# A seven-product linear layer with low-rank adapters: weight differences moved to GpSimd, loads of the first phase spread, and four smaller edits

## The reference

```python
result = jnp.einsum('bsd,od->bso', x, base_weight) + base_bias
A = lora_A_w[adapter_ids]
Bw = lora_B_w[adapter_ids]
h = jnp.einsum('bsd,brd->bsr', x, A)
lora_out = jnp.einsum('bsr,bor->bso', h, Bw)
result = result + lora_out
...
x = x + _L0_cond_ref(x, itok_B_6_15, L0_cond_base_weight, ...)
```

## Time and profile before

| | before |
|---|---|
| median of three runs | 1349.38 us |
| the profiled execution, its own time | 1349.27 us |
| its span, first to last instruction | 1347.5 us |
| mean granted TensorE clock | 0.994 of full |
| TensorE (matmul) busy | 1317.5 us, 98%, 7136 matmuls |
| VectorE busy | 594.5 us, 44% |
| ScalarE busy | 223.4 us, 17% |
| GpSimd busy | 191.9 us, 14% |
| DMA, mean over the span | 229 GB/s |

### The profile page before, as it was taken

One profiled execution on the slowest core, in us unless ns is written; L12 is line 12 of the kernel. 1 busy time (PEld: TensorE's weight loads), 2 busy tenths in 40 slices (PEclk: granted clock), 3 DMA queues, 4 the chain that ended last, 5 costly groups with the idle time before them and its releaser, 6 DMA issues.

```text
span 1347.5 us, 18275 instructions
## 1 busy us (share of the span) xinstructions
PE 1317.5 (98%) x7136; PEld 1208.9 (90%) x7136; DVE 594.5 (44%) x831; ACT 223.4 (17%) x408; POOL 191.9 (14%) x98
## 2 busy tenths in 40 slices
PE   7999979999999999999999999999999999999998
PEld 7999879999998888899999999999988888888886
DVE  4244345444545444564343645434644345533321
ACT  4111122111122000121111212111311111201110
POOL 0000012222220000022444522122100000000000
PEclk9999989999999999999999999999999999999999
DMA  5347767777688777746668755675566778855552
GB/s 199 130 151 264 235 240 283 265 257 255 237 274 287 249 253 266 295 161 239 240 240 301 268 202 151 196 217 194 177 231 237 252 257 299 291 188 196 197 193 102
DMA packets 93513, 308.78 MB, mean 229 GB/s; under 512 B 10482, under 2 KB 19746, under 8 KB 93474
## 3 DMA queue, kind: packets, MB, share of 16 engines
q1 hardware_dynamic: 93474, 308.35, 66.8%
HBM read 211.82 MB, written 97.01 MB: 229 GB/s over the span
## 4 chain that ended last, share of the span: by engine, by line
PE 87%; DMA 5%; DVE 4%; SPq 2%; ACT 1%; issue 1%; POOL 0%; DVEq 0%; ACTq 0%
PE acc L915 31%; PE acc L928 28%; PE acc L921 26%; PE acc L962 2%; DMA pool<-xT 2%; SPq L395 1%; DMA pool<-wT 1%; DVE h_keep L745 1%; DVE h_cols L751 1%; DMA w_sums<-pool 1%; DMA w_raw<-w_sums 1%; SPq L457 1%; POOL pool L854 0%; PE turned L951 0%; ACT x_hi L580 0%
## 5 line engine op out<-in xcount | busy, mean ns | idle before, releaser
L928 PE MATMUL acc<-w_lo,x_hi 128*128 128x352 f32 (+2 forms) x2304 | 566.0, 344 | 0.0
L928 PEld LDWEIGHTS acc<-w_lo,x_hi 128*128 128x128 f32 x2304 | 404.2, 189 | 33.2
L915 PE MATMUL acc<-w_hi,x_hi 128*128 128x352 f32 x1536 | 336.3, 327 | 19.9 <-DVE keep L780 11.7
L915 PE MATMUL acc<-w_hi,x_lo 128*128 128x352 f32 x1536 | 332.2, 324 | 0.0
L915 PEld LDWEIGHTS acc<-w_hi,x_hi 128*128 128x128 f32 x1536 | 258.9, 190 | 20.7 <-issue 12.4
L915 PEld LDWEIGHTS acc<-w_hi,x_lo 128*128 128x128 f32 x1536 | 264.6, 189 | 0.0
L921 PE MATMUL acc<-w_hi,x_hi 128*128 128x512 f32 x768 | 242.0, 396 | 0.1
L686 DVE TENSOR_TENSOR x_lo<-pool,x_hi 128x1024 fp32r<-128x1024 f32 x110 | 142.2, 1293 | 220.9 <-ACT x_hi L580 220.7
L921 PE MATMUL acc<-w_hi,x_lo 128*128 128x512 f32 x768 | 239.6, 392 | 0.0
L580 ACT ACTIVATE x_hi<-pool 128x1024 fp32r<-128x1024 f32 x110 | 116.2, 1056 | 706.8 <-PE acc L928 398.6
L786 DVE TENSOR_TENSOR pool<-acc,pool 128x352 f32<-128x352 f32 (+2 forms) x176 | 102.5, 635 | 184.6 <-PE acc L962 182.0
(11 more groups left out here) (35 smaller groups left out, 413.4 us busy)
## 6 DMA issues: line engine op xcount, KB each, us to landing
pool<-xT SPq DMA_DIRECT2D x142, 512.0 KB, 6.0
pool<-x SPq DMA_DIRECT2D x64, 512.0 KB, 5.7
out<-pool SPq DMA_DIRECT2D x48, 512.0 KB, 2.8
pool<-wT SPq DMA_DIRECT2D x32, 512.0 KB, 7.0
w_sums<-pool SPq DMA_DIRECT2D x32, 512.0 KB, 3.6
w_raw<-w_sums SPq DMA_DIRECT2D x32, 512.0 KB, 5.6
s_sums<-pool SPq DMA_DIRECT2D x32, 512.0 KB, 8.2
pool<-s_sums SPq DMA_DIRECT2D x32, 512.0 KB, 5.6
```

Of the source, the lines that this page charges most:

```text
L915: mm = nc.tensor.matmul(acc[j][:, o, 0:COLS_A], xs, w_hi[:, s, base + o * COLS_A:base + (o + 1) * COLS_A], start=(k == 0 and part == 0), s ...
L928: mm = nc.tensor.matmul(acc[j][:, o, low:low + n], x_hi[:, j, k], w_lo[:, slot(ph, k), first:first + n], start=False, stop=end and (ph not ...
```

## The change

Six edits:

1. The sets start at tile 2 + 3n instead of 4 + 3n, and all four differences are taken on GpSimd, the three behind `add_out` of their tile.
2. The pieces have a table of their own for when they are loaded and stored (`PIECE_LOAD`); each store follows the load by one tile.
3. The first four W chunks of the next phase are loaded one a tile, in tiles 11 to 14 of a phase, ahead of the set's loads.
4. In P1, P6 and P5 VectorE's `step` begins with the read-out of the tile before; it stood behind the splits of x and A.
5. The high and low columns of A change places (`HI_AT`, `LO_AT`), so that x_lo's product with the bank of the A columns can leave out the 16 low ones (336 columns instead of 352).
6. TensorE starts with 24 products of the unit matrix by itself. The last tile is written out: its `turn` and `low_rank` come after its chunks 5 and 6, its last chunk goes bank by bank, and each bank is read out and stored by itself.

```diff
+HI_AT = (RANK, AC + HALF)
+LO_AT = (0, AC + HALF + RANK)
-PREP_FROM = 4
+PREP_FROM = 2
+WARM = 24
+PIECE_LOAD = {(P1, 1): 0, (P1, 3): 1, (P1, 6): 2, (P1, 9): 3, (P1, 12): 4,
+              (P4, 2): 5, (P4, 4): 6, (P4, 6): 7, (P4, 8): 8}
+PIECE_SPLIT = {(ph, t + 1): n for (ph, t), n in PIECE_LOAD.items()}
+LAST_TURN, LAST_LORA = 5, 6
...
@@ SP, step(tile)
                 load_out(tile)
+                early = row(tile) - (2 * PEELED - 1)
+                if ph + 1 < len(PHASES) and 0 <= early < AHEAD:
+                    load_w_first(ph + 1, early)
                 chunk, part = prep_at(tile)
...
-                if j == 0 and piece_at(tile) is not None:
-                    load_piece(piece_at(tile))
+                if (ph, row(tile)) in PIECE_LOAD:
+                    load_piece(PIECE_LOAD[ph, row(tile)])
...
-                if ph + 1 < len(PHASES):
-                    load_w_first(ph + 1)
...
+            def store_last():
+                b = OUT_AT[P3][1][0]
+                for o in range(2):
+                    at = slice(o * BANK, (o + 1) * BANK)
+                    sp.wait_ge(acc_read, place(LAST) + o + 1)
+                    sp.dma_start(out[row(LAST):row(LAST) + 1, :, HALF + o * BANK:HALF + (o + 1) * BANK],
+                                 pool[:, b, at]).then_inc(pool_out[b], DMA)
@@ VectorE, step(tile)
+                if place(tile) and back.ph not in LORA_PHASES:
+                    read_out(back)
...
-                if place(tile):
+                if place(tile) and back.ph in LORA_PHASES:
                     read_out(back)
...
-                if prep_at(tile)[1] == 1:
-                    prep(prep_at(tile)[0])
@@ GpSimd (prep itself as on VectorE, with gp. and nc.gpsimd.)
                 if ph in ADD_PHASES:
                     add_out(tile)
+                if prep_at(tile)[1] == 1:
+                    prep(prep_at(tile)[0])
                 if prep_at(tile)[1] == 2:
                     prep_last(prep_at(tile)[0])
@@ TensorE
+                        ends = part == 1 and o == H_BANK[j]
+                        low, high = (0, COLS_A)
+                        if ends:
+                            low, high = (RANK, COLS_A) if j == 0 else (0, COLS_A - RANK)
+                        mm = nc.tensor.matmul(acc[j][:, o, low:high], xs,
+                                              w_hi[:, s, base + o * COLS_A + low:base + o * COLS_A + high],
...
+            def last():
+                back = after(LAST, -1)
+                begin(LAST)
+                for k in range(KC - 1):
+                    chunk(LAST, k)
+                    if k == TURN_AFTER:
+                        turn(back)
+                    if k == LORA_AFTER:
+                        low_rank(back)
+                    if k == LAST_TURN:
+                        turn(LAST)
+                    if k == LAST_LORA:
+                        low_rank(LAST)
...
+            pe.wait_ge(eye_filled, 3)
+            for _ in range(WARM):
+                nc.tensor.matmul(turned[:, 0:P], eye[:], eye[:], start=True, stop=True)
```

More of the change, by code:

```diff
@@ L525, in step @@
                     prep_store_last(chunk)
-                if j == 1 and piece_at(tile) is not None:
-                    store_piece(piece_at(tile))
+                if (ph, row(tile)) in PIECE_SPLIT:
+                    store_piece(PIECE_SPLIT[ph, row(tile)])
                 if tile == Tile(P1, 3, 0):
@@ L648, in step @@
                     h_high(tile)
-                if j == 1 and piece_at(tile) is not None:
-                    piece_high(piece_at(tile))
+                if (ph, row(tile)) in PIECE_SPLIT:
+                    piece_high(PIECE_SPLIT[ph, row(tile)])
                 if i >= PEELED and ph + 1 < len(PHASES):
@@ L809, in step @@
                     x_low(one)
-                if prep_at(tile)[1] == 1:
-                    prep(prep_at(tile)[0])
                 if ph in (P7, P3):
                     h_low(tile)
-                if j == 1 and piece_at(tile) is not None:
-                    piece_low(piece_at(tile))
+                if (ph, row(tile)) in PIECE_SPLIT:
+                    piece_low(PIECE_SPLIT[ph, row(tile)])
                 if i >= PEELED and ph + 1 < len(PHASES):
@@ L843, in _, with prep @@
                             step(Tile(ph, i, j))
[L844 removed]
+            b = OUT_AT[P3][1][0]
+            dve.wait_ge(pool_in[b], DMA * (LOADS[P3][b] + PAIRS))
+            for o in range(2):
+                rows = pool[:, b, o * BANK:(o + 1) * BANK]
+                dve.wait_ge(last_done, o + 1)
+                nc.vector.tensor_tensor(rows, acc[1][:, o], rows, ALU.add).then_inc(acc_read, 1)
         @block.gpsimd
         def _(gp):
+            def prep(n):
+                a, b, c = PREP_AT
+                gp.wait_ge(pool_in[a], DMA * (2 * n + 1))
+                gp.wait_ge(pool_in[b], DMA * (n + 1))
+                nc.gpsimd.tensor_tensor(pool[:, a], pool[:, b], pool[:, a], ALU.subtract).then_inc(w_summed, 1)
+                gp.wait_ge(pool_in[c], DMA * (n + 1))
+                gp.wait_ge(w_summed, 4 * n + 1)
+                nc.gpsimd.tensor_tensor(pool[:, b], pool[:, c], pool[:, b], ALU.subtract).then_inc(w_summed, 1)
+                gp.wait_ge(w_summed, 4 * n + 2)
+                nc.gpsimd.tensor_tensor(pool[:, c], pool[:, c], pool[:, a], ALU.subtract).then_inc(w_summed, 1)
             def prep_last(n):
@@ L914, in with_hi @@
                     for o in range(BANKS_A):
[L915 to L918, removed]
+                        ends = part == 1 and o == H_BANK[j]
[4 more added lines that the diff above has]
+                                              w_hi[:, s, base + o * COLS_A + low:base + o * COLS_A + high],
+                                              start=(k == 0 and part == 0), stop=(k == KC - 1 and ends))
                 else:
@@ L995, in _ @@
                         whole(Tile(ph, 0, j))
-                with pe.Fori(1, PAIRS) as i:
+                with pe.Fori(1, PAIRS - (ph == P3)) as i:
                     for j in range(2):
                         whole(Tile(ph, i, j))
-            turn(Tile(P3, PAIRS - 1, 1))
-            low_rank(Tile(P3, PAIRS - 1, 1))
+            whole(Tile(P3, PAIRS - 1, 0))
+            last()
 def kernel(x, itok_B_6_15, L0_cond_base_weight, L0_cond_base_bias, L0_cond_lora_A_w, L0_cond_lora_B_w):
```

64 lines of the change are left out of this document (30 added, 34 removed).

## The result

The changed kernel takes 1367.99 us (median of 4 runs, 1367.01 to 1368.49) against 1348.86 for the kernel before beside it: ratio 1.0144, interval 1.0126 to 1.0162. It is 19 us slower; forecast was 1338.2, with 8 chances in 10 for 1324 to 1353. The profiled execution spans 1366.7 us, with a mean clock of 0.986 (1347.5 and 0.994 before).

What follows compares the result with a forecast made beforehand. TensorE, busy 98% of the span, was taken as the bound, so only matmul columns or its few waits count. 5.7 + 1.8 + 1.9 + 1.7 = 11.1 us off 1349.27 gave 1338.2 us, 8 in 10 for 1324 to 1353.

Steps and rivals of the forecast that it cites:

- one P1 turn: 15.0 + 16.2 + 4.2 + 1.8 = 37.2 us: First phase, between set loads: loads to stores 15.0, stores to x load 16.2, piece stores 4.2, x to set loads 1.8.
- its own sign of being wrong, waits at tiles 13 to 16: TensorE waits already at tiles 13 to 16 would show the forecast wrong, with a time of 1350 and more.
- The rival with a binding chain: Slow landings make P1 turns 43.6 us, three turns add 19.2, so slower at 1357.4 us; chance 0.14.
- P2's turn: Second phase: set differences stand behind GpSimd's add, so a turn grows from 38.0 to 44.1 us.
- Tile 28 can start at 353.0: End of P2's chain: x for tile 28 goes out at 343.0, so it starts at 353.0 instead of 358.7.
- So 5.7 us are gained: Up to tile 28: 5.7 us gained, not P1's 16.1; the rest returns as x waits between tiles 21 and 28.
- The rival with P1's gain whole: SP stays ahead and P2 gets no new waits: 22.9 us gained, 1326.4 us; chance 0.30.
- The turned columns: TensorE's longest wait for turned low-rank columns, in tile 28, goes because the sets end at tile 25: 1.8 us gained.
- Columns: 512 x_lo products lose 16 of 352 columns, 6.5 ns each: 3.3 us in all, 1.9 counted; bounds 0 and 3.4.
- Unit-matrix products: At the start, 24 products under the first loads: taken as 0, a 3.5 us gap feared; bounds 0 and 2.5.
- The end: Last tile: moved turn and low-rank products 0.7, half a read-out 0.6, shorter last store 0.4; together 1.7 us gained.
- The shared port: In P2, GpSimd work slows VectorE and can hold the low-rank columns three times: counted 0, 5.4 us if not covered.

Runs made afterwards that it cites:

- run 1: Changed kernel with a set's three differences back on VectorE, all else as changed: 1330.62 us, ratio 0.9871 to the kernel before.
- run 3: Changed kernel with ScalarE writing h_stack before it splits the next x, in all low-rank phases: 1363.7 us, ratio 1.0107 to the kernel before.
- run 7: Kernel before with only the three differences moved to GpSimd, behind the add: 1376.44 us, ratio 1.0198 to the kernel before.
- 8: Kernel before with only the unit-matrix products, the narrower products and the last tile's new end: 1346.67 us, ratio 0.9987 to the kernel before.
- 10: Changed kernel with the differences on VectorE and the sets started at tile 4 instead of 2: 1328.34 us, ratio 0.9855 to the kernel before.
- run 2: Changed kernel with the sets started at tile 4 again, the differences still on GpSimd: 1351.3 us, ratio 1.002 to the kernel before.
- run 6: Changed kernel with P1's pieces loaded at rows 1, 4, 7, 10, 13, stored one row later: 1351.24 us, ratio 1.002 to the kernel before.
- 11: Changed kernel with the differences on VectorE and P1's pieces at rows 1, 4, 7, 10, 13: 1328.26 us, ratio 0.9847 to the kernel before.
- run 9: Changed kernel with GpSimd's differences ahead of the add and P1's pieces at rows 1, 4, 7, 10, 13: 1330.18 us, ratio 0.9868 to the kernel before.
- run 5: Changed kernel with a set's three differences ahead of the tile's add on GpSimd: 1345.48 us, ratio 0.9977 to the kernel before.

## Why the prediction was wrong

**The failed step: "one P1 turn: 15.0 + 16.2 + 4.2 + 1.8 = 37.2 us".** The chain was the right thing to count, and the forecast named the point itself: slower from a P1 turn of 40.9. Measured were 37.7, 40.4, 41.1 and 43.9. The worst term is the 1.8, from the x load to the set loads. In the third turn it is 5.9 (145.78 to 151.65), and over the last three turns it is 11.2 us too much, of the 13.8 by which they were longer than forecast. It was read at 103.11, where no 512 KB piece store stood ahead. Behind the very piece stores that gave the 4.2, at 132.64, the kernel before shows 4.2 for this way too, and 3.4 for issuing the three loads:

```profile
136.89 1.22 SPq L326 DMA_DIRECT2D pool<-xT  x1
...
141.05 3.41 SPq L481 DMA_DIRECT2D pool<-wT  x3
```

The 15.0, from loads to stores, is 17.1, because the loads were there 9.7 us after the first issue (110.55 to the first difference at 120.21), as in run 1 (109.48 to 119.22), and not after 7.6. About half of that is issue: the second load started at 112.27, 1.7 us after the first and not 0.6, and took 7.8 us from there. The 16.2 + 4.2 are 18.1 and gave 2.3 back. Set 4 came at 195.5 instead of 179.6. The x of tile 16 went out at 189.07 instead of 178 and landed after 11.5 us instead of 6.4, in a stretch where the DMA engines were 0.89 busy (ScalarE's timeline):

```profile
200.58 1.06 ACT L597 ACTIVATE x_hi<-pool 128x1024 fp32r<-128x1024 f32 x1 [19.50 <-DMA pool<-xT]
```

So 17.1 us were lost at the boundary where the forecast had none: its own sign of being wrong, waits at tiles 13 to 16. The rival with a binding chain had the P1 turn nearly right (43.6), by slower landings alone, but had P2 start from there without a further loss, and so stopped at 1357.4.

**P2's turn was right (44.1; 46.1 and 45.6), its consequence was too small.** The add ended 18.0 us after the set's loads, where the forecast had 17.7. "Tile 28 can start at 353.0" let x be late up to a tile's start. But ScalarE's h_stack stands behind the x split, so TensorE stops at the third chunk of the tile before; run 3 prices that at 5 us. Tile 28 started at 382.95 (its first low-rank instruction on VectorE, as 358.69 in the earlier trace rows), 30 us late. Set 7's loads had come 22 us late, at 324.05 instead of 301.9: 15.9 of it by set 4, 2.7 in the turn into P2, 3.5 in the two turns of P2. The other 8 us are that order, the half clock and what no run separates.

**"So 5.7 us are gained": credited to the wrong edit.** The forecast let the move take P1's wait away and counted the spread as worth nothing by itself. Runs 7, 8 and 10 say the reverse: the spread and the read-out order take all of it away (17.8 us), and the move alone, behind the add, makes the kernel 27 us slower. The move costs 22 us with the sets at tile 4 (run 2 against 10), 23 at tile 2 with the pieces moved (6 against 11), 37 as changed (against 1). The rival with P1's gain whole (1326.4) is near what runs 1, 9, 10 and 11 show, 1328 to 1331, with no large wait left; for the kernel as changed it was wrong. The early start wins nothing (10 against 1 and 11). With the differences on GpSimd it costs 15 to 17 where it puts the piece stores between two sets (5 against 9, as changed against 2 and 6); with them on VectorE that place costs 3 at most (1 against 11), within the intervals.

**The turned columns: 1.8 forecast, 3.7 measured** (4.7 to 1.0 us). The reason given, the earlier end of the sets, is not confirmed: in runs 9 and 11 the sets end as early, and these waits are 5.0 and 4.2 us.

**Columns: 3.3 forecast, 3.6 measured**, 319 ns instead of 326 on 512 products. After, for the 336 columns beside the 352 ones:

```profile
L944 PE MATMUL acc<-w_hi,x_lo 128*128 128x352 f32 x1024 | 251.4, 326 | 0.0
...
L944 PE MATMUL acc<-w_hi,x_lo 128*128 128x336 f32 x512 | 163.3, 319 | 0.0
```

**Unit-matrix products: 0 forecast, 1.2 measured.** The first groups in the chain after:

```profile
8.14 2.08 PE acc L944 x6
...
12.55 0.97 PE acc L944 x6
```

18 matmuls are done at 12.55, as at 13.77 before. The gap that the forecast feared was 0.9 us, since the products took 5.38 us, not 2.7 (TensorE's timeline after):

```profile
1.89 5.38 PE L1038 MATMUL turned<-eye 128*128 128x128 f32 x24 [1.89 <-POOL eye L919]
```

**The end: 1.7 forecast, 1.2 measured.** From the last regular matmul to the span's end it was 1347.5 - 1341.72 = 5.8 us; it is 4.1 (from 1362.62), but 0.5 of the difference is TensorE work that only moved.

```profile
1362.04 1.31 DVE L854 TENSOR_TENSOR pool<-acc,pool 128x512 f32<-128x512 f32 x2 [5.59 <-PE acc L1033]
1362.23 0.39 PE L1033 MATMUL acc<-w_lo,x_hi 128*128 128x512 f32 x1
```

**The shared port: 0 forecast, 5.4 as a bound.** The mechanism is in the timelines: of VectorE's 110 x splits after, the 74 that meet no operation of GpSimd take 1.23 us at most, and of the 36 that overlap one the longest takes 3.4. But their mean is not a measure of the move. Before, after, in run 1 (differences on VectorE) and in run 7 (the move alone), the mean ns behind the busy us:

```profile
L686 DVE TENSOR_TENSOR x_lo<-pool,x_hi 128x1024 fp32r<-128x1024 f32 x110 | 142.2, 1293 | 220.9 <-ACT x_hi L580 220.7
L703 DVE TENSOR_TENSOR x_lo<-pool,x_hi 128x1024 fp32r<-128x1024 f32 x110 | 168.1, 1528 | 106.3 <-ACT x_hi L597 106.3
L703 DVE TENSOR_TENSOR x_lo<-pool,x_hi 128x1024 fp32r<-128x1024 f32 x110 | 162.3, 1476 | 49.0 <-ACT x_hi L597 49.0
L686 DVE TENSOR_TENSOR x_lo<-pool,x_hi 128x1024 fp32r<-128x1024 f32 x110 | 141.1, 1283 | 256.1 <-ACT x_hi L580 256.1
```

The mean is 1528 ns after and 1476 in run 1, against 1293 before and 1283 in run 7. So it goes with how often a split falls beside some work of GpSimd, its adds too, and not with who takes the differences. Once the chain fits, run 9 against 11 gives 0.0021, 2.8 us, within their intervals: under the bound, and not told from nothing. The Trainium skill (GPSIMD Engine Reference, Engine selection) would give an elementwise operation on a tile to VectorE, with GpSimd about half as fast for two inputs. The rows agree on the ratio (2.40 us in run 5's fence, 1.21 in the earlier trace rows). On the time they agree only as far as someone waits for the difference: the slower engine itself costs 14 us in the chain of run 5 and 2.8 in run 9.

## What to carry to other kernels

When one engine issues transfers for several streams in one order, a step that only one stream waits for delays all of them: find that chain, count its turn from a stretch where the same transfers stand ahead, not from a quieter one, and compare it with the pace of what it feeds. Before work moves to an idle engine, look at what stands ahead of it in that engine's order and what that waits for; here the place behind the add cost 20 to 22 us (9 against 6, 5 against as changed). The slower engine itself cost 14 where the chain had no room and not more than 3 where it had. Test the edits of a bundle alone: here three of them won 18 us and another hid it with a loss of 37.

## Not expected of the hardware

Right behind a piece's three stores SP's own steps take longer. Three loads of 512 KB are issued in 3.45 us at 110.55 and 3.41 in the kernel before at 141.05. Where no piece's three stores stand just ahead it is 1.63 (at 103.11) and 1.28 (run 6's fence). Reading the adapter's number ahead of A's load takes 1.96 us at 147.01 (line 315), and 0.26 at the least in P1 and P2 of the same trace. Why the stores slow what follows them was not tested. The landing itself is less unusual: 7.8 us for the load that the first difference waited for, against 7.0 as the median before and 7.7 after.
